# AdaLN transformer block on one core: compact softmax divisors spread by small transfers, second normalisation on ScalarE

## The reference, cut to what matters

```python
h = layernorm(x) * (1 + ca) + sa                    # ca, sa, ga, cb, sb, gb from silu(c) @ wmod
Q, K, V = h @ wq, h @ wk, h @ wv                    # 16 heads of 8 channels
local = softmax(mask(Q K^T / sqrt(8))) V            # window of 32 tokens, blocks of 32 queries, 64 keys
GQ, GK, GV = h @ wgq, pool(h @ wgk), pool(h @ wgv)  # 8 heads of 8, 64 latents
rem = (softmax(lmask(GQ GK^T / sqrt(8))) GV) @ r_out_w
gl, gr = sigmoid(Q . gate_local_w), sigmoid(Q . gate_remote_w)    # one number per head and token
x = x + ga * ((gl * local + gr * rem) @ w_out)
h = layernorm(x) * (1 + cb) + sb
x = x + gb * ffn(h)        # per element mixed weights: W + sum_e g_e TW_e, with g from a small gate network
```

## Time and profile before

| | |
|---|---|
| device time, median of 3 runs (lowest, highest) | 776.82 us (775.74, 777.2) |
| the profiled execution: its own time | 776.43 us |
| its span, first to last instruction | 774.6 us |
| PE busy | 648.7 us, 84% |
| DVE busy | 609.0 us, 79% |
| ACT busy | 360.1 us, 46% |
| POOL busy | 287.3 us, 37% |
| mean granted TensorE clock | 0.976 of full speed |

### The profile page before, as it was taken

One profiled execution on the slowest core, in us unless ns is written; L12 is line 12 of the kernel. 1 busy time (PEld: TensorE's weight loads), 2 busy tenths in 40 slices (PEclk: granted clock), 3 DMA queues, 4 the chain that ended last, 5 costly groups with the idle time before them and its releaser, 6 DMA issues.

```text
span 774.6 us, 23963 instructions
## 1 busy us (share of the span) xinstructions
PE 648.7 (84%) x8822; PEld 508.4 (66%) x8822; DVE 609.0 (79%) x1305; ACT 360.1 (46%) x846; POOL 287.3 (37%) x350
## 2 busy tenths in 40 slices
PE   5687887888887887888778887888886999999998
PEld 3365655566655655666556655666656989898996
DVE  5568999999989999999998999999876637264542
ACT  2264455555545455555554555555541342432133
POOL 2357444455545444455554444455541000000000
PEclk9699999999999999999999999999987999999999
DMA  3767011001000111001000111000050010000001
GB/s 96 174 80 91 22 28 27 20 20 27 21 20 20 22 26 27 20 20 27 20 20 20 23 28 23 20 20 20 14 63 0 2 35 21 27 27 14 27 21 47
DMA packets 65797, 24.84 MB, mean 32 GB/s; under 512 B 38440, under 2 KB 64360, under 8 KB 65648
## 3 DMA queue, kind: packets, MB, share of 16 engines
q1 hardware_dynamic: 64320, 18.25, 10.1%
q0 software_dynamic: 1456, 6.31, 5.4%
HBM read 16.13 MB, written 8.40 MB: 32 GB/s over the span
## 4 chain that ended last, share of the span: by engine, by line
PE 41%; DVE 31%; issue 16%; POOL 8%; DVEq 2%; ACT 1%; DMA 0%; POOLq 0%; SPq 0%; ACTq 0%
DVE mx L545 10%; PE SB L809 7%; PE WB L797 7%; DVE xn_d L539 5%; DVE rden L623 5%; PE SB L916 4%; PE WB L784 4%; PE SB L784 4%; POOL rstd_a L327 3%; POOL rstd_d L327 3%; PE SB L871 2%; PE SB L920 2%; PE WB L959 2%; DVE st_a L530 2%; PE SB L983 2%
## 5 line engine op out<-in xcount | busy, mean ns | idle before, releaser
L334 POOL TENSOR_TENSOR KM<-K_ch,bd_scale 128x1024 f32<-128x1024 f32 x32 | 60.6, 1893 | 125.2 <-ACT K_ch L400 125.2
L545 DVE TENSOR_REDUCE mx<-SB 128x8 f32<-128x512 f32 x128 | 86.9, 679 | 1.5 <-PE SB L871 1.5
L392 ACT ACTIVATE Pr<-Pr 128x512 f32<-128x512 f32 x128 | 80.8, 631 | 10.8 <-DVE Pr L552 7.2
L490 ACT ACTIVATE Pr<-WB,mb1T 128x256 f32<-128x256 f32 x128 | 49.8, 477 | 75.7 <-PE WB L797 75.6
L552 DVE TENSOR_TENSOR Pr<-SB,mx 128x512 f32<-128x512 f32 x128 | 84.2, 678 | 0.0
L539 DVE TENSOR_SCALAR xn_d<-x_all,mv_d,rstd_d 128x128 f32 (+1 forms) x64 | 73.6, 1189 | 13.5 <-POOL rstd_d L327 13.5
L347 POOL TENSOR_TENSOR PT_sum<-PT 128x512 f32<-128x512 f32 x64 | 79.6, 1265 | 4.5 <-ACT PT L432 4.5
L623 DVE RECIPROCAL rden<-SB 128x256 f32<-128x256 f32 x32 | 56.2, 1757 | 14.3 <-PE SB L920 14.3
L432 ACT COPY PT<-SB 128x512 f32<-128x512 f32 x128 | 66.1, 622 | 0.0
L885 PE MATMUL SB<-ident,Pr 128*128 128x128 f32 x512 | 63.1, 277 | 0.7 <-ACT Pr L392 0.7
L809 PE MATMUL SB<-Pr,GA 128*128 128x256 f32 x256 | 61.2, 381 | 0.0
(11 more groups left out here) (192 smaller groups left out, 1503.5 us busy)
## 6 DMA issues: line engine op xcount, KB each, us to landing
x_all<-in_L_attn_x SPq DMA_DIRECT2D x32, 128.0 KB, 2.1
v_rows<-V_rows SPq DMA_DIRECT2D x32, 128.0 KB, 1.8
VBD<-v_rows SPq DMA_DIRECT2D x128, 32.0 KB, 1.9
TW<-in_L_ffn_TW POOLq DMA_DIRECT2D x16, 256.0 KB, 9.7
GA<-ga_rows POOLq DMA_DIRECT2D x1, 2048.0 KB, 11.8
out_x<-attT SPq DMA_DIRECT2D x16, 128.0 KB, 1.8
out_x<-y_ga SPq DMA_DIRECT2D x16, 128.0 KB, 1.8
PT<-in_L_ffn_W SPq DMA_DIRECT2D x2, 256.0 KB
```

The costliest lines, as they stand in the source:

```text
L392: nc.scalar.activation(Pr[:, k, :], Pr[:, k, :], ACT.Exp).then_inc(p_ready, 1)
L545: nc.vector.tensor_reduce(mx[:, k, :], SB[k][:].rearrange("p (h j) -> p h j", h=8), AX.X, ALU.max).then_inc(mx_ready, 1)
```

## The change

Four things are done together.

1. **Divisors in a compact layout.** The divisor matmuls use `quadG` and `quadL`, which sum each head into one row: 16 heads of 64 tokens in each quarter of the partitions, 64 columns instead of 256 (local) or 128 (latent). The reciprocals `den_c` and `lat_c` work on 64 columns. The gates are computed in the same layout: four matmuls of 64 columns, and a tanh `tg_c` over 64 columns.
2. **Spread by small transfers.** DVE multiplies the local gate into the reciprocal (`loc_c`). SP then spreads each compact row over the 8 channels of its head by transfers within SBUF: `lat_x` from `lat_c`, `loc_x` from `loc_c`, `tg_x` from `tg_c`, four transfers each. `rem_n`, `a_gated` and `rem_g` read the spread tiles.
3. **Second normalisation on ScalarE.** GpSimd computes -mean/std (`neg_d`, `shift_d`: two more operations) and ScalarE applies scale and shift (`xn_d`, two instructions ahead of `h2T`).
4. **Order and banks.** The local values are accumulated in WB[2] instead of SB[2]; the `rem` matmuls stand behind the transposes of `xn_a`; `rem_n` stands behind `loc_c`; `a_gated` and `rem_g` stand behind `PlA`, ahead of the first maximum.

The core of the diff:

```diff
@@ SP, step
+                if has(it, 2):
+                    b = it - 2
+                    sp.wait_ge(lat_ready, b + 1)
+                    for c in range(4):
+                        t, n = divmod(c, 2)
+                        sp.dma_start(lat_x[NL * t:NL * t + NL, n * CQ:(n + 1) * CQ],
+                                     bc(lat_c[W * c:W * c + LH, :], [LH, HD, CQ], 1)).then_inc(latx_loaded, 16)
+                if has(it, 1):
                     sp.wait_ge(v_stored, 16 * it)
                     sp.wait_ge(pv_done, it)
                     for h in range(4):
                         sp.dma_start(VBD[W * h:W * h + W, :, h, :], v_dram[:, h, :].rearrange("(k c) n -> c k n", c=W)
                                      ).then_inc(vbd_loaded, 16)
+                if has(it, 2):
+                    b = it - 2
+                    sp.wait_ge(loc_ready, b + 1)
+                    for c in range(4):
+                        sp.dma_start(loc_x[:, c * CQ:(c + 1) * CQ], bc(loc_c[W * c:W * c + H, :], [H, HD, CQ], 1)
+                                     ).then_inc(locx_loaded, 16)
+                if has(it, 1):
+                    b = it - 1
+                    sp.wait_ge(tg_ready, b + 1)
+                    for c in range(4):
+                        sp.dma_start(tg_x[:, c * CQ:(c + 1) * CQ], bc(tg_c[W * c + H:W * c + 2 * H, :], [H, HD, CQ], 1)
+                                     ).then_inc(tgx_loaded, 16)
@@ POOL, step
-                    inv_std(it - 4, aggr_d, mv_d, ve_d, eps_d, rstd_d, rstd_d_s)
+                    nc.gpsimd.tensor_tensor(ve_d[:], mv_d[:, :, 1], eps_row[:], ALU.add).then_inc(eps_d, 1)
+                    nc.gpsimd.tensor_tensor(neg_d[:], mv_d[:, :, 0], minus_one[:], ALU.mult).then_inc(neg_ready, 1)
...
+                    nc.gpsimd.tensor_tensor(shift_d[:], neg_d[:], rstd_d[:], ALU.mult).then_inc(shift_ready, 1)
@@ ACT, step
+                    act.wait_ge(shift_ready, b + 1)
+                    at_least(act, x2T_done, b)
+                    for t in range(T):
+                        nc.scalar.activation(xn_d[:, t, :], x_all[:, bass.ds(b * S + t * D, D)], ACT.Identity,
+                                             scale=rstd_d[:, t:t + 1], bias=shift_d[:, t:t + 1]).then_inc(xn_d_s, 1)
...
-                    nc.scalar.activation(tg[:].rearrange("p k s -> p (k s)"), WB[2][:], ACT.Tanh, scale=0.5
-                                         ).then_inc(tg_ready, 1)
+                    nc.scalar.activation(tg_c[:], WB[2][:, S:S + CQ], ACT.Tanh, scale=0.5).then_inc(tg_ready, 1)
@@ DVE, step
-                    nc.vector.reciprocal(rden[:], SB[2][:, S:2 * S]).then_inc(rden_ready, 1)
-                    dve.wait_ge(rden_ready, b + 1)
-                    nc.vector.tensor_tensor(a_loc[:], SB[2][:, 0:S], rden[:], ALU.mult).then_inc(a_ready, 1)
+                    nc.vector.reciprocal(den_c[:], WB[2][:, S + CQ:S + 2 * CQ]).then_inc(den_ready, 1)
+                    dve.wait_ge(den_ready, b + 1)
+                    dve.wait_ge(tg_ready, b + 1)
...
+                    nc.vector.scalar_tensor_tensor(loc_c[:], tg_c[:], 1.0, den_c[:], ALU.add, ALU.mult).then_inc(loc_ready, 1)
+                    dve.wait_ge(latx_loaded, N_X * (b + 1))
+                    at_least(dve, rem_done, b)
+                    nc.vector.tensor_tensor(rem_n[:], WB[0][:, 0:P], lat_x[:], ALU.mult).then_inc(remn_ready, 1)
...
                     latent_lowered(b, *latent_tiles[0])
+                if has(it, 2):
+                    b = it - 2
+                    dve.wait_ge(locx_loaded, N_X * (b + 1))
+                    at_least(dve, att_ready, b)
+                    nc.vector.tensor_tensor(a_gated[:], WB[2][:, 0:S], loc_x[:], ALU.mult).then_inc(ag_ready, 1)
+                    dve.wait_ge(rem_done, b + 1)
+                    dve.wait_ge(tgx_loaded, N_X * (b + 1))
+                    nc.vector.scalar_tensor_tensor(rem_g[:], tg_x[:], 1.0, WB[3][:, 0:S], ALU.add, ALU.mult
+                                                   ).then_inc(remg_ready, 1)
+                if has(it, 1):
+                    b = it - 1
                     maximum(b, 0)
@@ PE, values
                 for g in range(G):
-                    last = mm(SB[2][W * g:W * g + W, S:2 * S], ones_bd[:], PT_sum[:, g, :], start=False, stop=True,
-                              skip_group_check=True)
+                    for c in range(4):
+                        last = mm(WB[2][W * c:W * c + W, S + CQ:S + 2 * CQ], quadG[:, g, :], PT_sum[:, g, c * CQ:(c + 1) * CQ],
+                                  start=False, stop=(g == G - 1), skip_group_check=True)
```

More of the change, by code:

```diff
@@ L131, in adaln_block @@
         PL = sb("PL", [P, LG, S + P])
-        tg = sb("tg", [P, 2, S])
-        rden, a_loc, a_gated = sb("rden", [P, S]), sb("a_loc", [P, S]), sb("a_gated", [P, S])
-        rlden, rem_n = sb("rlden", [P, P]), sb("rem_n", [P, P])
+        tg_c, den_c, lat_c = sb("tg_c", [P, CQ]), sb("den_c", [P, CQ]), sb("lat_c", [P, CQ])
+        loc_c = sb("loc_c", [P, CQ])
+        tg_x, loc_x, a_gated = sb("tg_x", [P, S]), sb("loc_x", [P, S]), sb("a_gated", [P, S])
+        lat_x, rem_n = sb("lat_x", [P, P]), sb("rem_n", [P, P])
         rem_g = sb("rem_g", [P, S])
@@ L146, in adaln_block @@
         u = [Pr[:, 2 * k:2 * k + 2, :].rearrange("p a (c s) -> p (a c) s", s=S) for k in range(2)]
-        fT = [rden, a_loc]
+        fT = [loc_x, tg_x]
         o_sb = [attT, y_ga]
@@ L290, in _ @@
             step(B)
+            step(B + 1)
             with sp.Fori(0, NG) as g:
@@ L467, in after @@
                     act.wait_ge(gate_w_done, 1)
-                    for k in range(2):
-                        nc.scalar.copy(gate_w[:, k, :].rearrange("p (h d) -> p h d", d=HD),
-                                       bc(SB[2][:, k * H:(k + 1) * H], [P, H, HD], 2)).then_inc(gate_w_ready, 1)
+                    nc.scalar.copy(gate_w[:], SB[2][:, 0:2 * H]).then_inc(gate_w_ready, 1)
                 if it == 1:
@@ L603, in step @@
                     dve.wait_ge(lpv_done, b + 1)
[L604 to L607, removed]
+                    at_least(dve, latx_loaded, N_X * b)
+                    at_least(dve, remn_ready, b)
+                    nc.vector.reciprocal(lat_c[:], WB[0][:, P:P + CQ]).then_inc(lat_ready, 1)
                 if has(it, 1):
@@ L841, in projections @@
                     pe.wait_ge(ga_ready, 1)
-                    pe.wait_ge(gate_w_ready, 2)
-                for k in range(2):
-                    last = mm(WB[2][:, k * S:(k + 1) * S], gate_w[:, k, :], hT[:], start=True, stop=True)
+                    pe.wait_ge(gate_w_ready, 1)
+                for c in range(4):
+                    last = mm(WB[2][W * c:W * c + W, S:S + CQ], gate_w[:], hT[:, c * CQ:(c + 1) * CQ], start=True, stop=True)
                 last.then_inc(gates_done, 1)
@@ L929, in latent_values @@
                 pe.wait_ge(gvbd_ready, b + 1)
[L930 to L937 removed]
+                for k in range(2):
+                    for t in range(k, T):
+                        for g in range(LG):
+                            q = (LG * t + g) * W
+                            mm(WB[0][q:q + W, 0:P], GVBD[:, k, g, :], PL[:, g, (t + k) * P:(t + k + 1) * P],
+                               start=(k == 0), stop=(k == t), skip_group_check=True)
+                for k in range(2):
+                    for g in range(LG):
+                        for t in range(T - 1, k - 1, -1):
+                            for n in range(2):
+                                q, o = (2 * t + n) * W, (t + k) * P + n * CQ
+                                last = mm(WB[0][q:q + W, P:P + CQ], quadL[:, g, :], PL[:, g, o:o + CQ], start=False,
+                                          stop=(k == t and g == LG - 1), skip_group_check=True)
                 last.then_inc(lpv_done, 1)
@@ L986, in step @@
                     values(it)
-                    pe.wait_ge(remn_ready, it - 2 + 1)
-                    bank_free(pe, it, (3, yga_ready, 1, 1), (1, vrows_ready, 1, 1))
-                    for t in range(T):
-                        last = mm(WB[3][:, t * P:(t + 1) * P], r_out[:, t, :], rem_n[:], start=True, stop=True)
-                    last.then_inc(rem_done, 1)
                 if isinstance(it, int) and it == B + 3:
@@ L1008, in step @@
                     last.then_inc(xT_done, 1)
+                if has(it, 2):
+                    pe.wait_ge(remn_ready, it - 2 + 1)
+                    bank_free(pe, it, (3, yga_ready, 1, 1), (1, vrows_ready, 1, 1))
+                    for t in range(T):
+                        last = mm(WB[3][:, t * P:(t + 1) * P], r_out[:, t, :], rem_n[:], start=True, stop=True)
+                    last.then_inc(rem_done, 1)
                 if has(it, 1):
```

81 lines of the change are left out of this document (43 added, 38 removed).

## The result

The changed kernel takes **848.54 us** (median of four, 847.69 to 851.45) against 777.01 for the kernel before on the same chip: a ratio of 1.0926, 95% interval 1.0894 to 1.0959. The forecast was 799, range 775 to 816: slower was right, the size was three times too small. The profiled execution spans 846.5 us (before 774.6) at a mean granted clock of 0.933 (before 0.976). A run more than 1.5% above the fastest of its kernel is left out of the ratios; that is one run, of experiment 5.

What follows compares the result with a forecast made beforehand. DVE's order, with TensorE close behind, was taken to set the 17.24 us step. The 28 loop steps at -0.67 + 1.26 = +0.59 gave +16.5; with +5.5 and +0.7 elsewhere, 22.7 on 776.43 made 799 us, range 775 to 816.

Steps and rivals of the forecast that it cites:

- E: Point in a loop step where local values and divisors are done and `rden` starts; forecast to come 0.67 us earlier.
- From the copies to E: From the end of ScalarE's `PT` copies through `xn_d`, transposes, values and divisors: 0.67 us earlier a step.
- From E to the first maximum: From divisors through SP's `VBD` and `loc_x` issues to DVE's first score maximum: 5.70 us against 4.44, so 1.26 later.
- Covered work: Latent and tanh spreads, loads of `x`, smaller gate work in a loop step: hidden behind other work, costed at nothing.
- the `lat_x` term: Four issues and landing spreading `lat_c`, about 3.2 us: SP through with them before the values end, no cost.
- The clock: Rival: longer TensorE idle after the scores lowers its granted clock; 0 to 2.1 us a step, 833 us; 9 in 100.
- The edges: Set-up and steps outside the 28 full loop steps (2, 3, 32, 33, last two): +5.5 and +0.7 us together.
- The faster rival: Transfers within SBUF land in about 1.2 us, issues take 0.30, spread hidden: -0.40 a step, 768 us; 8 in 100.
- Its floor: First maximum no earlier than 4.95 us after the values end, set by TensorE's `rem` matmuls and scores, whatever transfers cost.
- the slow rival: TensorE's granted clock falls in every step after about 2.1 us idle: +34 us at 1.2 a step, 833; 9 in 100.

Runs made afterwards that it cites:

- experiment 5: The changed kernel with the four `loc_x` transfers copying the 128 rows of `loc_c` as they lie, output not the reference's: 848.3 us, ratio 1.0921.
- experiment 4: The changed kernel with 16 transposes that nobody reads in TensorE's idle stretch ahead of the projections, loop steps only: 834.2 us, ratio 1.0747.
- experiment 1: The kernel before with only the second normalisation moved to ScalarE, GpSimd's two added operations included: 748.7 us, ratio 0.9639.
- experiment 3: The changed kernel with SP's four `loc_x` issues moved ahead of its four `VBD` issues: 800.6 us, ratio 1.0314.

## Why the prediction was wrong

The same step in each kernel, and what each difference isolates:

| kernel | loop step, us | time, us | the difference to the line above |
|---|---|---|---|
| before | 17.24 | 776.8 | |
| `xn_d` on ScalarE | 16.35 | 748.7 | -0.89: E earlier |
| and compact layout, spread free | 16.79 | 771.9 | +0.44: `rem_n` behind the values |
| and spread, ahead of `VBD` | 17.48 | 800.6 | +0.69: issues and landing |
| and spread behind `VBD`, TensorE kept busy | 18.56 | 834.2 | +1.08: SP's queue |
| as changed | 19.04 | 848.5 | +0.48: clock, then `lat_x` ahead of `VBD` |

Point by point, by the prediction's own steps:

- **From the copies to E: right.** Forecast 0.67 earlier, measured 0.88. `xn_d` took 0.93 (0.92 forecast) but starts under the tail of the copies' record, so transposes begin 0.82 after the copies and not 0.96; the divisors cost +0.03, not +0.09.
- **From E to the first maximum: right mechanism, terms too small.** Forecast 5.70, measured 6.65 in the short step. The wait behind `VBD` was right (SP begins `loc_x` 1.91 after E, forecast 1.84). From the first `loc_x` issue to the last were 1.90, forecast 3 x 0.45 = 1.35: an issue of the spread takes 0.60, and no row of before showed one, so the price of `VBD` was taken. The landing was 2.1 to 2.2, forecast 1.85. The upper bound of the sum, 6.2, did not hold the 6.65: both prices were bounded by rows of other transfers (up to 0.46 and 2.3), and an issue lay outside its bound. The Trainium skill ("DMA: Bandwidth & Descriptors", section "Anatomy of one DMA", which is about transfers that GpSimd issues) has about 2.0 for a transfer's set-up and completion. The landings of 2.1, of transfers that SP issues, lie nearer to it than to the 1.85.
- **Covered work: the `lat_x` term failed.** It was costed at nothing, with SP "through with them before E". In the short step SP is through 0.25 us before E, so the cover was that thin. In the long step they run 0.6 past E, and `VBD` and `loc_x` start 0.8 late. The issues took 2.65 together, against the 1.8 that `VBD`'s price makes.
- **The clock: a rival with 9 in 100, and it came on top.** The prediction held it against the forecast; it happened together with it, since a longer wait on `loc_x` makes the idle stretch longer (2.6, forecast 2.1). Its price was 0.48 a step in the mean, inside the 0 to 2.1 given, and it went through `lat_c` and SP's queue rather than through transposes and values.
- **The edges: +6.2 forecast, about +26 measured.** 8.5 of it are TensorE's two stalls, and no step of the prediction asked what a longer TensorE program meets beside the expert loads. Over steps 2 to 4 the granted clock is 0.81 (before 0.94), which no term of the forecast held either; how the other 18 us divide was not measured. Just ahead of the first stall, a store of `v_rows` and a load of `x` landed after 8.3 and 9.0 us (2.0 and 2.1 in the median).
- **The faster rival: its premise was wrong.** Landing 2.1 and issue 0.60, not 1.2 and 0.30; no landing of `loc_x`, within SBUF, was below the median of 1.8 of `VBD`, which reads from DRAM, so leaving out DRAM gained nothing here. Its floor, E + 4.95, was right (4.86), and with free transfers the time is 771.9 (forecast 768): -0.45 a step where -0.40 was forecast, and dearer edges.

So +0.59 a step became +1.80 (1.68 in the mean, since two steps of the kernel before took 18.7): -0.21 for E, +0.95 for issue and landing, +0.48 for the clock and `lat_x`. Without the last of these the 834.2 of experiment 4 is still above the range. The range missed because its two ends moved the same terms alone; that the slow rival and the forecast could both hold was not in it.

## What to carry to other kernels

When an instruction is made cheaper by a layout that has to be spread by transfers, price the way from tile to tile as a queue: who stands ahead on the issuing engine, how many issues, one landing; here 1.2 us were saved on the reciprocal and 4.0 us of issues and landing put after it. The order of waits in one issuing queue was worth 48 us, and costs nothing to choose. A change of two parts is measured part by part: here one part was worth -28 us and the other, on top of it, +100.

## What the runs showed of the hardware that was not expected

- A transfer from tile to tile holds SP for 0.60 us per issue (0.45 for `VBD`, of the same 32 KB); reading 16 rows eight times each adds 0.3 us to the landing (2.1 against 1.8) and nothing to the issue.
- TensorE's granted clock stays at 1.00 in the loop with idle stretches ahead of the projections of 1.4 to 1.5 us (experiment 1) and 1.6 to 1.7 (experiment 3). It falls in 16 of 27 steps with 2.5 to 2.8 (the changed kernel); sixteen transposes in the gap took it back and made the kernel 14 us faster.
- A 32 KB transfer issued while eight experts' weights are being loaded took 25 us instead of 2.1.
- TensorE can stop for 1.6 to 4.5 us in the middle of a row of matmuls with no wait in the profile (the longest in experiment 5). Here it did so at the end of expert loads, in steps 3 and 4 of kernels with more matmuls; with the loads moved it did not. What holds it is not shown.
